# One-core AdaLN block with attention: both weighted-sum steps placed together behind a block's second score pair

## What is computed

```python
scores = jnp.einsum('bhqd,bhkd->bhqk', q, k) / math.sqrt(hd)
causal = jnp.tril(jnp.ones((l, l), bool))
scores = jnp.where(causal, scores, -jnp.inf)
att = jax.nn.softmax(scores, axis=-1)
out = jnp.einsum('bhqk,bhkd->bhqd', att, v)
```

## Time and profile before

| | |
|---|---|
| time, median of 3 runs | 2920.46 us (2919.89 to 2921.38) |
| profiled execution | 2918.9 us, its span 2917.2 us |
| PE busy | 2764.7 us (95%) |
| DVE, ACT, POOL busy | 1578.7 (54%), 1058.9 (36%), 1281.3 us (44%) |
| mean granted PE clock | 0.979 of full speed |

### The profile page before, as it was taken

How to read it: one execution, slowest core, us unless ns; L and a number is a source line. 1 busy time by engine, 2 the same in 40 slices (tenths; PEclk the granted TensorE clock), 3 DMA queues, 4 the chain that set the end, 5 groups by cost and what they waited for, 6 DMA issues and landing times. The chain is left out here.

```text
span 2917.2 us, 41697 instructions
## 1 busy us (share of the span) xinstructions
PE 2764.7 (95%) x16180; PEld 2009.6 (69%) x16180; DVE 1578.7 (54%) x3165; ACT 1058.9 (36%) x1446; POOL 1281.3 (44%) x672
## 2 busy tenths in 40 slices
PE   4999999999999999889999999999999958999997
PEld 2888888888888888645555555555555527888886
DVE  4232223222323122267887777777777726777775
ACT  1322322122113111245666656556565631112121
POOL 2322332242225111267777777777777741212120
PEclk8999999999999999899999999999999979999998
DMA  7444343334335644365555555555555244544541
GB/s 250 161 159 160 140 181 134 140 116 173 116 115 169 213 164 168 127 138 121 117 117 118 122 127 127 118 126 127 128 121 117 67 146 142 148 148 138 166 130 58
DMA packets 153996, 404.85 MB, mean 139 GB/s; under 512 B 21820, under 2 KB 57076, under 8 KB 152776
## 3 DMA queue, kind: packets, MB, share of 16 engines
q1 hardware_dynamic: 123480, 292.05, 29.4%
q10 hardware_dynamic: 30320, 110.15, 17.7%
HBM read 270.41 MB, written 131.20 MB: 138 GB/s over the span
## 5 line engine op out<-in xcount | busy, mean ns | idle before, releaser
L1093 ACT ACTIVATE prob<-ps_s 128x1024 f32<-128x1024 f32 (+3 forms) x768 | 597.2, 810 | 407.2 <-PE ps_s L1231 390.4
L787 PE MATMUL ps_u<-h_hi,w_hi 128*128 128x512 f32 x1536 | 612.5, 399 | 2.0 <-POOL h_lo L555 2.0
L787 PE MATMUL ps_u<-h_lo,w_hi 128*128 128x512 f32 x1536 | 601.3, 391 | 0.0
L787 PE MATMUL ps_u<-h_hi,w_lo 128*128 128x512 f32 x1536 | 600.0, 391 | 0.0
L1049 POOL TENSOR_TENSOR added<-added,prob 128x2048 f32<-128x2048 f32 (+1 forms) x128 | 550.5, 4301 | 4.6
L549 POOL TENSOR_TENSOR w_lo<-w_raw,w_hi 128x1024 fp32r<-128x1024 f32 x93 | 222.6, 2393 | 473.1 <-ACT w_hi L617 473.1
L678 DVE SCALAR_TENSOR_TENSOR qk_lo<-ps_u,bias_col,qk_hi 128x512 fp32r<-128x512 f32 x128 | 96.0, 750 | 578.9 <-ACT qk_hi L593 578.9
L1135 DVE TENSOR_REDUCE part_high<-ps_r 128x1 f32<-128x512 f32 x496 | 330.6, 686 | 88.1 <-PE ps_r L1201 88.1
L1131 DVE CUSTOM_DVE_ANT_0 ps_r<-ps_r,row_mask 128x384 f32<-128x384 f32 (+1 forms) x500 | 312.5, 630 | 108.7 <-PE ps_r L1201 107.6
L1201 PE MATMUL ps_r<-k_st,q_st 96*128 96x512 f32 (+1 forms) x1008 | 330.9, 386 | 16.8 <-DMA v_sb<-v_tok 9.0
L787 PEld LDWEIGHTS ps_u<-h_lo,w_hi 128*128 128x128 f32 x1536 | 288.7, 188 | 61.6
(11 more groups left out here) (197 smaller groups left out, 3429.6 us busy)
## 6 DMA issues: line engine op xcount, KB each, us to landing
w_raw<-w_cols SPq DMA_DIRECT2D x72, 512.0 KB, 6.2
qk_split<-qk_hi SPq DMA_DIRECT2D x64, 512.0 KB, 2.6
qk_split<-qk_lo SPq DMA_DIRECT2D x64, 512.0 KB, 4.1
q_st<-qk_split ACTq DMA_DIRECT2D x60, 512.0 KB, 7.5
k_st<-qk_split ACTq DMA_DIRECT2D x60, 512.0 KB, 13.6
xn<-in_L_attn_x SPq DMA_DIRECT2D x8, 2048.0 KB, 12.8
v_tok<-v_out SPq DMA_DIRECT2D x32, 512.0 KB, 4.4
wm<-in_L_wmod SPq DMA_DIRECT2D x8, 2048.0 KB, 8.0
```

The source lines that it names most:

```text
L787: last = nc.tensor.matmul(ps_u[u % 2][:], w[:, m, k], h[:, k, tok], start=k == 0 and j == 0, stop=k == KT - 1 and j == 2)
L1093: nc.scalar.activation(prob[:, buffer_of(t, k), 2 * pair:2 * pair + 2, off:], ps_s[pair][:, :, off:], ACT.Exp, scale=SCALE).then_inc(exp_d ...
```

## The change

The second `weigh` of each of the blocks 2 to 5 moves from the end of the block to right behind the first one, after the block's second score pair. Nothing stands at the block's end. The rows are dealt anew around it; their order and their number in a block stay as they are. It holds for all 32 passes; the first pass has shares of its own, which stay.

```diff
-    SHARES = ((2, 1, 1, 1, 1), (2, 2, 2, 2, 1), (2, 1, 2, 2, 1), (2, 1, 2, 1, 1), (2, 1, 2, 2, 1), (1, 1, 1, 1, 0))
+    SHARES = ((2, 1, 1, 1, 1), (2, 2, 2, 2, 1), (1, 2, 1, 2, 2), (1, 2, 1, 1, 2), (1, 2, 1, 2, 2), (1, 1, 1, 0, 1))
...
             def rest(t, p, half):
 
-                if p >= HOPS:
-                    weigh(t, 2 * (p - HOPS) + half)
+                if p >= HOPS and half == 0:
+                    weigh(t, 2 * (p - HOPS))
+                    weigh(t, 2 * (p - HOPS) + 1)
+                elif p >= HOPS:
+                    return
                 elif t > 0 and (p, half) == (0, 0):
```

## The result

The changed kernel takes 2938.9 us (median of 4 runs, 2938.1 to 2944.9) against 2920.6 us before (2919.9 to 2921.4): a ratio of 1.0067, with a 95% interval of 1.0049 to 1.0084. It is slower by 18.3 us. The profiled execution of after took 2938.05 us, its span is 2936.2 us, and its mean granted clock of PE is 0.979, as before.

What follows compares the result with a forecast made beforehand. PE sets the pace, DVE close behind. 0.2 + 0.3 us a pass less 0.15 gives 0.35, times 30 is 10.5 us: 2918.9 becomes 2929.4, and with 1.6 for the median 2931 us; range 2911 to 2943.

Steps and rivals of the forecast that it cites:

- What merging gives PE: Weighed-sum steps on PE: each merged pair saves 0.32 us, four pairs a pass, 41 us if nothing else became late.
- What it takes from DVE: Blocks 2 to 4: three banks hold under 1.9 us of DVE's work, so DVE reaches the shift 1.2 us later.
- The shift: Second half's shift, L1148 and SP's four transfers: the fourth starts at 1798.7 and lands between 1800.1 and 1800.7.
- The rival that the large loads hold the shift back: Pass's end: ACT's large loads still run when the shift is sent, another 0.6 us a pass, 2949 us; chance 0.05.
- First scores: Start of the next pass's first scores on PE: at 1800.4 to 1800.7, taken as 1800.5, 0.2 us later.
- The end of the pass: Next pass's third row: waits 0.2 us for its bank and pays 0.1 for a weight load, 0.3 us; bounds 0 to 0.4.
- the deduction of 0.15 us a pass: Average pass: a PE waiting for DVE anyway hides part of the 0.23 us of irregular waits; 0.15 taken off.
- First and last pass: First pass has other shares, last almost no rows: both put at 0, between -2 and +2.
- The signs: Right: merged groups 1.84 and 1.64 us, more weight-load waits for DVE, period 35.2 to 35.5; wrong: rows waiting less for DVE.
- That DVE keeps up: Rival, blocks 2 to 4: rows are read faster than taken, so PE gets the saved drains, 2901 us; chance 0.18.
- That losses and gains cancel: Rival: the shift lands in PE's shadow and the end costs nothing, within 0.2 us of a pass, 2921 us; chance 0.24.
- The rule of the Trainium skill on drains: Weighed-sum steps: changing tiling mode drains the engine, changing tile within a mode does not; by it alone 2879 us.

Runs made afterwards that it cites:

- the light kernel with small loads: Changed kernel with single-head row reductions reading half the columns, and q, k, v loads bringing a quarter of theirs from the sixth group on: 2880.8 us.
- the light kernels: Kernel before and changed kernel, each with single-head row reductions reading half of the columns: 2907.7 us without the change, 2910.3 with it.

## Why the forecast held

The forecast was 2931.0, slower, within 2911 to 2943; measured were 2938.9. The way and the mechanism came as forecast; of the size, 10.5 us were forecast and 18.3 found. Point by point:

- **What merging gives PE.** A pair of 512 columns was taken at 1.84 us and is 1.85 in the median; 512 + 384 at 1.64, and it is. The saving is real, and the light kernel with small loads has use for it. In the whole change it is lost.
- **What it takes from DVE.** This was the heart of the forecast, and its times up to the shift's last issue came out within 0.05 us (medians against one walked pass): DVE goes on 0.89 and 1.10 us later than before behind the first two pairs, the third pair starts 0.48 us later, and the shift is made 1.45 us later. That it is DVE's rate is shown by the light kernels, where the price of the change goes from 18 to 2.6 us.
- **The shift.** I had bounds of 30.1 to 30.7 us, measured against my pass as 29.8 to 30.4, and it lands at 30.11. For the forecast that was enough, but there is luck in it. The lower bound, 1.4 us behind the last issue, was read from the last byte moved in a pass whose shift landed at 29.71, 2.5 us behind that issue. The 2.0 us that the prediction cites from the Trainium skill (DMA: Bandwidth & Descriptors) are a fit there on transfers issued by GpSimd; these are SP's, and 1.6 us were measured. What I had no eye for is that before the change the issue's time didn't set the landing: the loads did. The rival that the large loads hold the shift back came out the other way round. They hold the landing in the kernel before and in the light ones; after the change their last packets move at 28.9, 0.4 us behind the start of the shift's last issue and before that transfer's own packets.
- **First scores: 0.2 us forecast, 0.3 in the walked pass's terms.** They start 30.31 us behind the sums, 0.31 after those of my pass (30.00), 0.22 after the median of before. In the typical pass PE is not stopped by the shift there: in the pass behind the one shown it lands 0.13 us later, at 30.22, and the first scores start at 30.31 all the same. DVE stops it, where the walk had put no wait: the row at 1771.08 waits 0.18 us in block 5, and the weights of the row right ahead of the first scores are loaded 0.27 us late (PEld, 1775.04).
- **The end of the pass: 0.3 us forecast, 0.29 found.** From the first scores to the third row it is 0.65 us instead of 0.46 (the wait of 0.2), and that row takes 0.28 instead of 0.18 (the weight load of 0.1). Everything behind it takes as long as before. The two kernels with half of the change show that this needs both: with the merging alone the stretch from the first scores to the next sums is 4.82 us, with the shares alone 4.74, after the whole change 5.04, before 4.74 (medians).
- **The sizes that were off.** The walk gave 0.5 us a pass where 0.6 were found, from 34.74 to 35.34: 3 us of the 6 by which the thirty passes exceed the forecast (16.6 against 10.5). The next is one that the sum had no term for: the pass of 37.63 us with PE's clock at 0.50, 2.2 us above the mean of the other 29. The last is the deduction of 0.15 us a pass. I held that a PE which waits for DVE anyway would hide part of the irregular waits. Without that pass the mean period is longer than the typical one by 0.115 us (35.455 against 35.34), where it was 0.23: it hid 0.12, and 1 us is missing. The mean of all thirty, 35.53, would have made it look as if it hid only 0.04. The deduction was the one term for which I had no row.
- **First and last pass.** I put them at 0, between -2 and +2: +2.5 us ahead of the first sums, of which 1.1 us were there before attention began, and -0.1 behind the 31st.
- **The signs.** Merged groups, idle stretches of DVE (1.79, 1.65, 1.24 forecast as 1.3 to 1.9), the shift at 26.2, the third row's wait and a period of 35.2 to 35.5 came as I had said (35.34 in the typical pass, 35.53 on the mean, just past the end). One failed as I had put it, and it stood among the signs of being wrong too: in the list the waits of PE's weight loads put down to DVE fell. The list counted the idle time behind each weighed-sum step among them; without it they rose, from 23.2 to 87.5 us.
- **The rivals.** That DVE keeps up is false at its full work. That losses and gains cancel fell with the two places above. The rule of the Trainium skill on drains (TensorEngine Tiling (Array Packing), Key Properties) fits what is measured (a merged pair holds PE for 1.85 us, two single steps for 0.99 each), and by itself said 2879, wrong by 60 us: a saving on the busiest engine is worth only what the next limit leaves of it.

## What to carry to other kernels

Where one engine fills a few buffers and another empties them, grouping the first one's other work makes a pause longer than the buffers can bridge: here three rows, 1.9 us of DVE's work, against the 3.0 us of a score pair, a merged pair and the next row (0.47 + 0.09 + 1.84 + 0.63). Count that before counting what the grouping saves. And before a small transfer is issued sooner, look at what else is moving when it lands: if its landing doesn't follow its issue from one pass to the next, it is the other traffic that has to be moved. Last, read a mean together with its single passes and its clock by stretches: one pass in thirty made an eighth of what the thirty lost, and a mean clock of 0.979 on both sides hid it.

## What I had not expected of the hardware

- A 2 KB transfer whose issue starts anywhere from 25.4 to 27.2 us lands at 29.6 to 29.8 us (medians of six kernels; single passes 28.8 to 31.0) while another queue's seven loads of 512 KB end at 28.9. With a quarter of those loads it lands 1.6 to 1.8 us behind its issue.
- Issuing half of the transfers on another queue, 1.2 us sooner, moved nothing (0.9997, 0.9988 to 1.0005).
- Putting the seven loads ahead of the shift in the same queue made its landing earlier by 0.5 us, not later.
- PE's granted clock fell to 0.50 in single passes behind idle stretches of 0.5 to 1.9 us, in every traced kernel with merged steps and in none without; in the changed kernel it was one pass, 2.2 us longer than the others.
